# rstd of three layer norms moved from GpSimd to ScalarE, and hosted steps placed anew

## What is computed

```
# layer 0: attention inside 64 x 64 diagonal blocks, an MLP, a layer norm
Wh = x @ W;  e = leaky(Wh @ a, 0.2)
S = softmax(adj[64-blocks on the diagonal] * e, axis=-1);  o = S @ Wh
y = leaky(leaky(o @ W1 + b1) @ W2 + b2) @ W3 + b3;  z = y + o
z = (z - mean(z)) / sqrt(var(z) + 1e-5) * ln_g + ln_b
x = layernorm(x + z)
# layer 1: dense attention, 4 heads of 32
h = x @ W_proj.T
s = leaky(s_left[i] + s_right[j] + adj[i,j] * we, 0.2), masked where adj <= 1e-5
agg = softmax(s, over j) @ h
x = layernorm(x + leaky(x + agg + bias, 0.5))
```

## Time and profile before

| | us |
|---|---|
| median of 3 runs | 2187.94 (2185.88 to 2188.89) |
| the profiled execution | 2188.64 |
| its span, first to last instruction | 2186.8 |

### The profile page before, as it was taken

One profiled execution on the slowest core, in us unless ns is written; L12 is line 12 of the kernel. 1 busy time (PEld: TensorE's weight loads), 2 busy tenths in 40 slices (PEclk: granted clock), 3 DMA queues, 4 the chain that ended last, 5 costly groups with the idle time before them and its releaser, 6 DMA issues.

```text
span 2186.8 us, 33731 instructions
## 1 busy us (share of the span) xinstructions
PE 1853.5 (85%) x10854; PEld 869.1 (40%) x10854; DVE 1898.1 (87%) x3667; ACT 1548.6 (71%) x3095; POOL 2063.9 (94%) x1050
## 2 busy tenths in 40 slices
PE   6588888888898888988889888888879888888785
PEld 4444434444343433443444443444434343333332
DVE  1189889899898999988999888989889899999997
ACT  6677777776867767777676776777777776666663
POOL 2499999999999999999999999999999999999996
PEclk8689999999999999999999999999999999999998
DMA  3223323324233332323323323323324323243320
GB/s 91 66 85 97 89 71 110 90 78 116 64 100 99 83 92 82 110 77 95 97 87 107 83 64 115 90 85 102 93 68 110 90 78 102 64 111 92 87 78 10
DMA packets 138480, 191.64 MB, mean 88 GB/s; under 512 B 22205, under 2 KB 56385, under 8 KB 138305
## 3 DMA queue, kind: packets, MB, share of 16 engines
q1 hardware_dynamic: 138304, 189.49, 30.2%
HBM read 180.82 MB, written 8.65 MB: 87 GB/s over the span
## 4 chain that ended last, share of the span: by engine, by line
POOL 45%; issue 22%; DVE 15%; PE 14%; ACT 3%; SPq 1%; DVEq 0%; POOLq 0%; DMA 0%; ACTq 0%
POOL X L456 36%; PE psum L998 11%; DVE X L914 11%; POOL rstd L411 2%; PE psum L1149 2%; DVE X L908 2%; POOL x1s L425 2%; POOL erstd L411 1%; POOL x1s L426 1%; POOL xb L407 1%; ACT E L694 1%; POOL nmu L412 0%; DVE psum L884 0%; POOL lg L410 0%; PE psum L1076 0%
## 5 line engine op out<-in xcount | busy, mean ns | idle before, releaser
L456 POOL TENSOR_TENSOR X<-RHO,E 128x1536 f32<-128x1536 f32 x512 | 1755.9, 3463 | 23.1 <-ACT E L694 23.1
L914 DVE SCALAR_TENSOR_TENSOR X<-psum,s_j,X 128x512 f32<-128x512 f32 x2048 | 1393.8, 744 | 169.0 <-POOL X L456 152.0
L998 PE MATMUL psum<-X,haug 128*33 128x512 f32 x4096 | 1016.1, 618 | 5.9 <-DVE X L914 3.2
L694 ACT ACTIVATE E<-psum,we_s 128x512 f32<-128x512 f32 x512 | 398.7, 779 | 512.7 <-PE psum L998 510.6
L1149 PE MATMUL psum<-ident,adj_sb 128*128 128x128 f32 x2048 | 438.2, 294 | 235.8 <-DVE X L914 234.8
L1149 PEld LDWEIGHTS psum<-ident,adj_sb 128*128 128x128 f32 x2048 | 290.7, 142 | 713.1 <-DVE X L914 608.4
L699 ACT ACTIVATE psum<-psum,we_s 128x512 f32<-128x512 f32 x512 | 382.1, 746 | 0.0
L998 PE MATMUL psum<-sgn_ident,pen 128*128 128x128 bf16 x2048 | 381.7, 221 | 0.0
L998 PEld LDWEIGHTS psum<-X,haug 128*33 128x33 f32 x4096 | 199.9, 113 | 455.7 <-issue 416.1
L661 ACT ACTIVATE pen<-adj_sb,pen_bias 128x512 bf16<-128x512 f32 x512 | 370.4, 724 | 0.7
L908 DVE TENSOR_TENSOR X<-psum,E 128x512 f32<-128x512 f32 x512 | 346.4, 677 | 17.1 <-ACT psum L527 17.1
(11 more groups left out here) (178 smaller groups left out, 1370.7 us busy)
## 6 DMA issues: line engine op xcount, KB each, us to landing
adj_sb<-in_adj_dram SPq DMA_DIRECT2D x128, 1024.0 KB, 5.1
RHO<-rho_scratch SPq DMA_DIRECT2D x32, 1024.0 KB, 9.4
out_dram<-o_sb SPq DMA_DIRECT2D x32, 256.0 KB, 5.7
xg<-in_x_dram SPq DMA_DIRECT2D x28, 256.0 KB, 5.6
blk<-in_adj_dram SPq DMA_DIRECT2D x56, 64.0 KB, 5.3
X<-in_x_dram SPq DMA_DIRECT2D x2, 256.0 KB, 2.8
W_sb<-in_L_gnn_W_dram SPq DMA_DIRECT2D x4, 64.0 KB, 1.9
X<-in_adj_dram SPq DMA_DIRECT2D x4, 64.0 KB, 2.8
```

Of the source, the lines that this page charges most:

```text
L456: Q.tensor_tensor(X[m % NX][:, 0:HP, :], RHO[:, g % 2, 0:HP, :], bc(E[m % NE][:], 1, [P, HP, GROUP]), ALU.mult).then_inc(B_pool, 1)
L694: A.activation(E[m % NE][:], TA[m % NT], ACT.Exp, scale=we_s[:, 3:4], bias=we_s[:, 5:6]).then_inc(E_sb, 1)
L914: ins = V.scalar_tensor_tensor(slot[:, h, :], TA[m % NT], s[:, k, h:h + 1], slot[:, h, :], ALU.mult, ALU.max)
L998: return T.matmul(o, l, r, start=start, stop=stop)
```

## The change

rstd is computed on ScalarE as exp(-0.5 ln(var + eps)); ScalarE also negates the mean, and GpSimd keeps one product, shift = -mean * rstd (`z_shift`, `r_shift`, `epi_shift`). Three more semaphores carry the step on from GpSimd. One activation table set is loaded ahead of everything. The slots: PREP and the last chain's z, residual, r and TAIL steps one later, one HEAD step and the softmax steps later, two XB later; the epilogue's norm from k = 13 to 15, its store from 14 to 15. Ahead of the loop the four z rstd stand before z's norms on ScalarE, and the four r rstd before the logits of the next two chains.

```diff
-    HEAD = ((-22, -21, -20), (-19, -18, -17), (1, 3, 5), (14, 16, 17))
+    HEAD = ((-22, -21, -20), (-19, -18, -17), (1, 3, 6), (14, 16, 17))
-    TAIL = ((13, 14, 15), (26, 27, 28), (38, 39, 40), (49, 50, 51))
-    Z = [mid[5] for mid in MID]
-    XB = (-20, -12, 12, 24)
+    TAIL = ((13, 14, 15), (26, 27, 28), (38, 39, 40), (50, 51, 52))
+    WH = [head[2] for head in HEAD]
+    ZS = (3, 15, 28, 41)
+    XB = (-20, -12, 15, 26)
-    PREP = 53
+    PREP = 54
@@ GpSimd
-            def invstd(var, out, shifted, mean_var):
-                link(Q.tensor_tensor(var[:], mean_var[:, :, 1], eps_c[:], ALU.add))
-                link(Q.tensor_tensor(out[:], var[:], mhalf[:], ALU.pow))
-                link(Q.tensor_tensor(shifted[:], mean_var[:, :, 0], out[:], ALU.mult))
-            def z_rstd(c):
+            def z_shift(c):
                 v = set_of(c)
-                pool.wait_ge(var_z, GT * (c + 1))
-                if c >= NB + 2:
-                    pool.wait_ge(x1_sb, prev(c) + 1)
-                invstd(lg[v], rstd[v], nmu[v], mv[v])
-                Q.tensor_scalar(shift[v][:], nmu[v][:], -1.0, None, ALU.mult).then_inc(rstd_z, 1)
+                pool.wait_ge(rstd_z, c + 1)
+                Q.tensor_tensor(shift[v][:], nmu[v][:], rstd[v][:], ALU.mult).then_inc(shift_z, 1)
...
-                        if n == Z[u] + 6:
-                            z_rstd(c)
-                        if n == Z[u] + 9:
+                        if n == ZS[u] + 4:
+                            z_shift(c)
+                        if n == ZS[u] + 6:
                             residual(c)
-                        if n == Z[u] + 12:
-                            r_rstd(c)
+                        if n == ZS[u] + 9:
+                            r_shift(c)
...
-                if k == 11 and g > 0:
-                    epi_rstd(g - 1)
+                if k == 12 and g > 0:
+                    epi_shift(g - 1)
@@ ScalarE
+            def invstd(log, out, minus, mean_var):
+                A.activation(log, mean_var[:, :, 1], ACT.Ln, bias=eps_c[:])
+                link(copy(minus, mean_var[:, :, 0], -1.0))
+                return A.activation(out, log, ACT.Exp, scale=-0.5)
+            def z_rstd(c):
+                v = set_of(c)
+                act.wait_ge(var_z, GT * (c + 1))
+                invstd(lg[v][:], rstd[v][:], nmu[v][:], mv[v]).then_inc(rstd_z, 1)
...
-                        if n == HEAD[u][2] + 4:
+                        if n == WH[u] + 5:
                             chain_logits(c)
-                        if n == HEAD[u][2] + 8:
+                        if n == WH[u] + 9:
                             chain_exp(c)
-                        if n == HEAD[u][2] + 11:
+                        if n == WH[u] + 13:
                             chain_soft(c)
...
+                        if n == ZS[u] + 3:
+                            z_rstd(c)
-                        if n == Z[u] + 8:
+                        if n == ZS[u] + 5:
                             z_norm(c)
-                        if n == Z[u] + 13:
+                        if n == ZS[u] + 8:
+                            r_rstd(c)
+                        if n == ZS[u] + 10:
                             r_norm(c)
...
+            A.preload_act_table_set("natural_log_exp_and_others")
...
-                    if k == 13:
+                    if k == 11:
+                        epi_rstd(g - 1)
+                    if k == 15:
                         epi_norm(g - 1)
@@ VectorE
-                        if n == HEAD[u][2] + 5:
+                        if n == WH[u] + 6:
                             chain_max(c)
-                        if n == HEAD[u][2] + 9:
+                        if n == WH[u] + 11:
                             chain_rin(c)
-                        if n == Z[u] + 3:
+                        if n == ZS[u]:
                             z_stats(c)
-                        if n == Z[u] + 9:
+                        if n == ZS[u] + 6:
                             r_stats(c)
```

More of the change, by code:

```diff
@@ L82, in build_program @@
         tiny = sb("tiny", [P, 1])
-        eps_c = sb("eps_c", [P, GT])
-        mhalf = sb("mhalf", [P, GT])
+        eps_c = sb("eps_c", [P, 1])
         pen_bias = sb("pen_bias", [P, 1])
@@ L241, in build_program @@
         rstd_z = sem("rstd_z")
+        shift_z = sem("shift_z")
         zn_sb = sem("zn_sb")
@@ L245, in build_program @@
         rstd_r = sem("rstd_r")
+        shift_r = sem("shift_r")
         x1_sb = sem("x1_sb")
@@ L291, in build_program @@
         erstd_sb = sem("erstd_sb")
+        eshift_sb = sem("eshift_sb")
         o_done = sem("o_done")
@@ L382, in _ @@
                     load_rho(g + 1)
-                if k == 14 and g > 0:
+                if k == 15 and g > 0:
                     store_out(g - 1)
@@ L426, in residual, with r_shift @@
                 Q.tensor_tensor(x1_of(c)[:], x1_of(c)[:], xb[s], ALU.add).then_inc(r_sb, 1)
-            def r_rstd(c):
+            def r_shift(c):
                 v = set_of(c)
-                pool.wait_ge(var_r, GT * (c + 1))
-                invstd(lg[v], rstd[v], nmu[v], mv[v])
-                Q.tensor_scalar(shift[v][:], nmu[v][:], -1.0, None, ALU.mult).then_inc(rstd_r, 1)
+                pool.wait_ge(rstd_r, c + 1)
+                Q.tensor_tensor(shift[v][:], nmu[v][:], rstd[v][:], ALU.mult).then_inc(shift_r, 1)
             def make_haug(nb, q):
@@ L441, in make_haug, with epi_shift @@
                                 bc(v_j[:, rows], 3, [P, CHUNK, H, DH]), ALU.mult).then_inc(haug_sb, 1)
[L443 to L447, removed]
+            def epi_shift(g):
+                pool.wait_ge(erstd_sb, g + 1)
+                Q.tensor_tensor(eshift[:], enmu[:], erstd[:], ALU.mult).then_inc(eshift_sb, 1)
             def tile(m):
@@ L491, in _ @@
             Q.memset(eps_c[:], EPS)
-            Q.memset(mhalf[:], -0.5)
             pool.drain()
@@ L515, in _ @@
                 host(m)
-                if k == 11 and g > 0:
-                    epi_rstd(g - 1)
+                if k == 12 and g > 0:
+                    epi_shift(g - 1)
                 tile(m)
-            epi_rstd(NG - 1)
+            epi_shift(NG - 1)
         @block.scalar
@@ L590, in chain_zc, with r_rstd @@
                 copy(x1_of(c)[:].rearrange("p t f -> p (t f)"), mid_bank(c)).then_inc(zc_sb, 1)
+            def invstd(log, out, minus, mean_var):
[6 more added lines that the diff above has]
+                invstd(lg[v][:], rstd[v][:], nmu[v][:], mv[v]).then_inc(rstd_z, 1)
+            def r_rstd(c):
+                v = set_of(c)
+                act.wait_ge(var_r, GT * (c + 1))
+                invstd(lg[v][:], rstd[v][:], nmu[v][:], mv[v]).then_inc(rstd_r, 1)
             def norm(dst, src, scale, bias_):
@@ L599, in z_norm @@
                 v = set_of(c)
-                act.wait_ge(rstd_z, c + 1)
+                act.wait_ge(shift_z, c + 1)
                 norm(x1_of(c), x1_of(c), rstd[v], shift[v]).then_inc(zn_sb, 1)
@@ L604, in r_norm @@
                 v = set_of(c)
-                act.wait_ge(rstd_r, c + 1)
+                act.wait_ge(shift_r, c + 1)
                 norm(x1_of(c), x1_of(c), rstd[v], shift[v]).then_inc(x1_sb, 1)
@@ L682, in epi_prelu, with epi_rstd @@
                 A.activation(BK_B, res[:].rearrange("p t f -> p (t f)"), ACT.Prelu, alpha=0.5).then_inc(prelu_ps, 1)
+            def epi_rstd(g):
+                act.wait_ge(evar, GT * (g + 1))
+                invstd(elog[:], erstd[:], enmu[:], emv).then_inc(erstd_sb, 1)
             def epi_norm(g):
-                act.wait_ge(erstd_sb, g + 1)
+                act.wait_ge(eshift_sb, g + 1)
                 act.wait_ge(out_st, 16 * g)
@@ L727, in host @@
                             chain_y2(c)
-                        if n == Z[u] + 3:
+                        if n == MID[u][5] + 3:
                             chain_zc(c)
-                        if n == Z[u] + 8:
+                        if n == ZS[u] + 3:
+                            z_rstd(c)
+                        if n == ZS[u] + 5:
                             z_norm(c)
-                        if n == Z[u] + 13:
+                        if n == ZS[u] + 8:
+                            r_rstd(c)
+                        if n == ZS[u] + 10:
                             r_norm(c)
@@ L782, in _ @@
                 penalty(m)
+            for c in U:
+                z_rstd(c)
             for c in (NB, NB + 1):
@@ L821, in _ @@
             epi_prelu(NG - 1)
+            epi_rstd(NG - 1)
             epi_norm(NG - 1)
@@ L849, in z_stats @@
                 if c >= NB + 2:
-                    dve.wait_ge(rstd_r, prev(c) + 1)
+                    dve.wait_ge(shift_r, prev(c) + 1)
                 stats(st6[s], mv[s], lambda t: x1_of(c)[:, t, :], var_z)
@@ L891, in epi_stats @@
                     dve.wait_ge(o_done, g)
-                    dve.wait_ge(erstd_sb, g)
+                    dve.wait_ge(eshift_sb, g)
```

## The result

The changed kernel takes 2148.1 us (median of 4 runs, 2144.0 to 2149.4) against 2186.9 of the kernel before on the same chip: ratio 0.982, 95% interval 0.980 to 0.984. It is faster, as forecast, but by 39 us and not by 110: 18 us above the top of the range.

What follows compares the result with a forecast made beforehand. GpSimd alone was taken to set the pace, 262.4 us per middle body. Bodies of 246.9 (floor 239.9 plus 7 of stalls) save 108.6, last body 3.6, after the loop 0.9, before it +3.3: 2079 us, range 2060 to 2105.

Steps and rivals of the forecast that it cites:

- Moved steps: Steps put in other slots: GpSimd finds the rstd done, cost 0; RHO's transfer one slot later, 0 to 1 us per body.
- the small stalls: GpSimd held up by late E at several slots of each body: 7 us per body, between 1 and 15.
- slot 3: Start of each body: TensorE's transposes, z and old products delay ScalarE's accU and E, 2.4 us against 1.92 before.
- ScalarE's heap at 31: ScalarE's piled-up steps at slots 15 (zc, exp, epilogue norm) and 31: together 1.0 us per body.
- the other slots from 25 to 45: VectorE's hosted lumps make it late: stall 0.4 us at slot 25, 0.9 for slots 36 to 42.
- slot 59: VectorE's epilogue parts and statistics at slots 52 to 58 make it late: stall 1.0 us per body.
- slack of 2.04: How late E may reach GpSimd, in us, before GpSimd's product stalls; VectorE's lateness was carried against it slot by slot.
- What lies outside the bodies: Before the loop +3.3 us (2 to 6), after the loop -0.9, last body -3.6.
- the floor of 239.9: GpSimd's work per body in us once each rstd leaves one product there; VectorE 236.8 and TensorE 231.2 lie within 4%.
- last body: Final body, nearly without hosted work: VectorE's lumps decide, 223.1 us against 226.7 before.
- Rival 1: Small stalls grow until TensorE and ScalarE bind: 15 us of stalls, body 255, 2136 us; chance 0.22.
- Rival 3: Pinned table set fails, ScalarE reloads 24 times per body: 22 us more per body, 2233 us, slower; chance 0.04.

Runs made afterwards that it cites:

- Experiments 1: Changed kernel with the store of RHO, and RHO's load behind it, ahead of the adjacency load of its slot on SP: 2117.0 us, ratio 0.968.
- experiment 9: Store first, accumulator copy behind E of tile 3, PREP back to 53 and the last chain's steps in old slots: 2113.4 us, ratio 0.966; repeated 2114.4.
- experiment 8: Changed kernel with the store first, the residual's multiplication by ln_g on GpSimd left out: 2090.7 us, ratio 0.955.
- experiment 6: Changed kernel with the store first, without the activation table set loaded ahead: 2279.9 us, ratio 1.042.
- experiment 3: Kernel before with the arithmetic of the change alone, all slots as before: 2137.3 us, ratio 0.977.
- (4): Kernel before with the slots of the change alone, rstd still four operations on GpSimd: 2228.9 us, ratio 1.019.
- experiment 2: Kernel before with only the store of RHO on SP one slot later, behind the adjacency load: 2232.7 us, ratio 1.021.

## Why the prediction was wrong

The step that failed stands under *Moved steps*: "Price 0, up to 1 per body where it lands late" for the RHO transfer. It measured 6.1 per body, 42.8 us. I had the date (15.5 us ahead, 9.4 to land) and the slot's 4.4, but moved the transfer in time only. In SP's queue it was moved past another transfer, and that adds what SP waits for there (5.3 us) and the longer landing behind 1 MB (5.3 instead of 1.8): 6.1 - 4.4 - 5.3 - 3.5 = -7.1, against 6.7 measured. I named the queue for the store of the output and did not do it for the line next to it. Experiments 1 and 2 show it from both sides. With the store in order the kernel takes 2117.0: of the 70 us that the forecast of 2079 was off this order is worth 31 by experiment (43 by the wait, 12 of which other stalls then take), and the rest would have lain inside the range.

The second term is the small stalls. Forecast 7 per body (1 to 15), measured 10.3 beside RHO, 11.7 with the store first: 3 to 5 us per body more, 23 to 33 us. By place: slot 3 forecast 2.4, 2.3 (3.3 with the store first, where the long stall no longer covers it); slots 14 to 19 with ScalarE's heap at 31 2.0 in all, 2.6; the other slots from 25 to 45 1.3, 3.0; slot 59 1.0, 1.4; slot 51 nothing, 1.1. (The working for slot 3, 1.92 + 0.9 + 0.67 - 1.0, gives 2.5 and not the 2.4 put down; VectorE's tile is 3.21 by its rows and not 3.23. Neither moves the sum by 1 us.) The reckoning of lateness against a slack of 2.04 found the places, and came out short where two sources add up and at 51, the accumulator copy of the fourth group, which I had looked at for slot 19 alone. Part of the stalls comes and goes with TensorE's granted clock (the end of experiment 9), for which the forecast had no term.

The seven full bodies took 1794.8 (107.55 to 1902.33) against a forecast of 1724.8, which is the whole error of 70: 42.8 for RHO, 23 for the small stalls, and 4 that I did not place (gaps too short for the table). What lies outside the bodies came out as forecast in sum.

What held: GpSimd set the pace (the floor of 239.9 is 240.0 busy), though not alone, for only 64% of a further cut came through (experiment 8); per rstd 0.16 instead of 1.90 on GpSimd (forecast 0.17); 0.53 on ScalarE (0.55); one table load; the shift never waited in a middle body; first tile 107.5 (forecast 109.7; 109.4 with the store first); last body 225.3 (223.1). Rival 1 gave the nearest time (2136, 257.6 instead of 255 per body), and that is luck: its 15 us of stalls per body are 16.6, but 6.2 of them are the order on SP, which it does not have. The other 10.3 are stalls of its kind, GpSimd behind E, and E behind TensorE or behind what ScalarE has to do first. Rival 3 was right that a missing pin turns the gain into a loss (2280; its 22 us per body on top of kernel 1 make 2271), and here too the parts were wrong where the sum was near: a load is 1.30 in the loop and not 2.06, and instead a rstd of 3.2 us holds up both E and its own shift. The Trainium skill (ScalarE: Activation LUTs, What ACT_TABLE_LOAD costs) gives about 2.66 us per switch with its drain; the rows of experiment 6 show 1.30, and by the larger figure it would have been about 2370, an estimate. The Trainium skill (ScalarE: Activation LUTs, Table sets: the hidden batching unit) says to batch calls by set: that agrees, with 162 us for reloading between Ln and Exp (experiment 6). It also counts one load for ln followed by exp; experiment 6 shows two per rstd where no set is loaded ahead, and one load in the whole program where it is.

## What to carry to other kernels

When a step with a transfer moves by one slot, write down the order of its queue before and after, with what each entry waits for: a slot is a date, but the queue decides. After an engine that was alone at its limit is relieved, price the stalls place by place (its lateness against the slack, and every step on other engines that waits for the end of a group), and take their sum as a lower value; here the stalls were 10 to 12 us per body, after 2 before, against 21 taken off GpSimd. Undo the parts of a change one at a time: the arithmetic alone was 11 us faster than the whole change (experiment 3), the slots alone 42 slower (4), and one line of order hid 31 us of what both are worth together (1). And look at several bodies of a profile, with the granted clock beside them, before you read a difference of 1 or 2 us per body between two kernels.

## What the runs showed of the hardware that I had not expected

A 32 KB store issued right behind a 1 MB load landed after 5.3 us (4.8 in experiment 2), and after 1.8 where no load stood right in front of it. A table load between two ScalarE operations takes 1283 ns, 1.30 us from start to start, the same 1283 as the first one with nothing before it. The same stretch of the same program ran at a granted TensorE clock of 1.00, 0.88 or 0.78 in different bodies of one execution, and GpSimd's wait at its end was 0.52, 2.12 or 3.71 us.
